# The order of GpSimd's queue around the last routed groups of a mixture-of-experts kernel

## The reference

```python
y = einsum('bct,bcd->bdt', x, cond_w[itok])        # 4096 tokens x 1024
logits = y @ W_gate + b_gate
_, top_idx = top_k(logits, 2)
y_all = relu(einsum('bsd,edh->bseh', y, W_e) + b_e)
out = x + take_along_axis(y_all, top_idx[..., None], axis=2).mean(axis=2)
```

## Time and profile before

| | us |
|---|---|
| median of 3 runs (893.49 to 895.28) | 893.74 |
| profiled execution | 893.59 |
| its span | 891.5 |
| TensorE busy | 851.7 |
| GpSimd busy | 511.1 |
| VectorE busy | 412.4 |
| ScalarE busy | 256.8 |

### The profile page before, as it was taken

One profiled execution on the slowest core, in us unless ns is written; L12 is line 12 of the kernel. 1 busy time (PEld: TensorE's weight loads), 2 busy tenths in 40 slices (PEclk: granted clock), 3 DMA queues, 4 the chain that ended last, 5 costly groups with the idle time before them and its releaser, 6 DMA issues.

```text
span 891.5 us, 16451 instructions
## 1 busy us (share of the span) xinstructions
PE 851.7 (96%) x4104; PEld 674.6 (76%) x4105; DVE 412.4 (46%) x548; ACT 256.8 (29%) x310; POOL 511.1 (57%) x559
## 2 busy tenths in 40 slices
PE   7899896999999999999999999999999999999992
PEld 3445475888878888888888888888888888888882
DVE  5688864356643373335533373336333733333320
ACT  5566310133511252113311331115111511222210
POOL 2266777767566756564665556555655566555411
PEclk9999997999999999999999999999999999999997
DMA  8999999878965586446854595547654564444333
GB/s 283 418 413 400 375 306 311 255 223 259 293 148 113 113 273 149 100 94 161 231 104 91 99 298 102 110 97 214 167 114 98 183 129 100 90 98 101 71 48 47
DMA packets 53065, 162.35 MB, mean 182 GB/s; under 512 B 13307, under 2 KB 13819, under 8 KB 53019
## 3 DMA queue, kind: packets, MB, share of 16 engines
q0 software_dynamic: 26464, 76.74, 40.0%
q1 hardware_dynamic: 20298, 67.91, 21.2%
q10 hardware_dynamic: 6272, 17.34, 4.9%
HBM read 106.73 MB, written 70.42 MB: 199 GB/s over the span
## 4 chain that ended last, share of the span: by engine, by line
PE 76%; DMA 14%; DVE 3%; issue 2%; POOL 2%; ACT 0%; POOLq 0%; ACTq 0%; SPq 0%; DVEq 0%
PE psO L573 73%; DMA rows<-in_x 5%; PE psO L513 2%; DMA out<-rows,first_to 1%; DMA out<-in_x 1%; DMA first<-slot_table 1%; DMA out<-ys,first_to 1%; DMA out<-ys,idx_s 1%; DMA slot_table<-toks,idx_all 1%; DMA rows<-y_rows,idx_g 1%; POOL slot_table L391 1%; POOL rows L419 1%; DVE turned L821 1%; DMA out<-rows,idx_s 1%; DMA wgc<-in_L_ffn_W_gate 1%
## 5 line engine op out<-in xcount | busy, mean ns | idle before, releaser
L573 PE MATMUL psO<-w_hi,a_hi 128*128 (+1 forms) x1104 | 342.0, 391 | 1.0 <-DVE a_lo L971 1.0
L573 PE MATMUL psO<-w_lo,a_hi 128*128 (+1 forms) x1104 | 340.8, 390 | 0.0
L573 PE MATMUL psO<-w_hi,a_lo 128*128 (+1 forms) x1104 | 340.4, 390 | 0.0
L419 POOL DMA_INDIRECT rows<-y_rows,idx_g x248 | 257.1, 1037 | 106.6 <-issue 52.4
L573 PEld LDWEIGHTS psO<-w_lo,a_hi 128*128 128x128 f32 x1104 | 207.8, 188 | 43.4
L573 PEld LDWEIGHTS psO<-w_hi,a_lo 128*128 128x128 f32 x1104 | 207.6, 188 | 43.3
L573 PEld LDWEIGHTS psO<-w_hi,a_hi 128*128 128x128 f32 x1104 | 207.0, 188 | 44.1 <-issue 1.8
L971 DVE TENSOR_TENSOR a_lo<-ys,a_hi 128x1024 fp32r<-128x1024 f32 x62 | 75.9, 1225 | 112.1 <-ACT a_hi L704 112.1
L692 ACT ACTIVATE ys<-ys 128x1024 f32<-128x1024 f32 x33 | 35.0, 1061 | 262.5 <-DVE ys L933 262.5
L692 ACT ACTIVATE rows<-rows 128x1024 f32<-128x1024 f32 x33 | 35.0, 1060 | 250.3 <-DVE rows L933 250.3
L933 DVE TENSOR_TENSOR ys<-psO,bias 128x1024 f32<-128x1024 f32 x33 | 40.3, 1222 | 130.9 <-PE psO L573 108.4
(11 more groups left out here) (129 smaller groups left out, 330.2 us busy)
## 6 DMA issues: line engine op xcount, KB each, us to landing
raw<-in_L_ffn_W_e SPq DMA_DIRECT2D x56, 512.0 KB, 6.3
rows<-in_x SPq DMA_DIRECT2D x32, 512.0 KB, 8.8
y_rows<-ys ACTq DMA_DIRECT2D x32, 512.0 KB, 8.7
out<-in_x SPq DMA_DIRECT2D x14, 1024.0 KB
bias<-in_L_ffn_b_e SPq DMA_DIRECT2D x8, 512.0 KB, 8.5
rows<-y_rows,idx_g POOLq DMA_INDIRECT x248
raw<-in_L_ffn_W_e POOLq DMA_DIRECT2D x4, 512.0 KB, 8.6
bias<-in_L_ffn_W_e POOLq DMA_DIRECT2D x4, 512.0 KB, 8.3
```

Source lines behind the costliest of these rows:

```text
L419: pool.indirect_dma_start(out=rows[:, slot, a * DQ:(a + 1) * DQ], out_offset=None, in_=y_parts[0:(1 + TOK) * Q, :], in_offset=bass.Indirec ...
L573: last = nc.tensor.matmul(ps[:, h * BANK:(h + 1) * BANK], a[:, p, k * P:(k + 1) * P], w[:, bass.ds(slot + (k * H + h * BANK), BANK)], star ...
```

## The change

No instruction is added or taken away; five programs are put in another order. GpSimd does the whole of route(3) ahead of early(0), then route(4) ahead of early(1) and so on, all seven early fetches and the gathers of tiles 7 and 8 ahead of any scatter, and then four scatters in a row. SP's reads for tiles 5 and 6 stand behind fewer copies. TensorE's share(5) and share(6) run at k = 5 of tiles 2 and 3. ScalarE loads the table ahead of relu(3) and early_hi(5). VectorE turns tile 4 ahead of finish_early(2), and its `schedule`, idx_all and finishes stand elsewhere among the early steps.

```diff
@@ sync
                 read_first(4)
-                for c in range(2, 7):
-                    copy(c)
+                copy(2)
+                copy(3)
                 read_first(5)
-                for c in range(7, 11):
+                for c in range(4, 8):
                     copy(c)
                 read_first(6)
-                for c in range(11, len(left)):
+                for c in range(8, len(left)):
                     copy(c)
@@ gpsimd
                 route(1)
                 route(2)
-                route(3, range(1))
+                route(3)
                 early(0)
-                route(3, range(1, 2))
+                route(4)
                 early(1)
-                route(4)
+                route(5)
                 early(2)
-                route(5)
+                route(6)
                 early(3)
-                pool.wait_ge(s_pad, 16)
-                scatter_early(0)
-                route(6)
                 early(4)
+                route(7)
                 early(5)
-                scatter_early(1)
-                route(7)
                 early(6)
-                scatter_early(2)
                 for s in range(G):
                     pool.wait_ge(s_xout[s], 16 * (len(STORES) // G))
                 pool.wait_ge(s_idx, 1)
                 gather(tile(0, EARLY))
                 gather(tile(0, EARLY + 1))
-                scatter_early(3)
+                pool.wait_ge(s_pad, 16)
+                for t in range(4):
+                    scatter_early(t)
                 regather(tile(0, 9))
@@ tensor
-                early_products(2, hooks={2: lambda: share(5)})
-                early_products(3)
-                early_products(4, hooks={0: lambda: share(6)})
+                early_products(2, hooks={5: lambda: share(5)})
+                early_products(3, hooks={5: lambda: share(6)})
+                early_products(4)
@@ scalar
                 early_hi(3)
+                early_hi(4)
                 relu(tile(0, 2))
-                early_hi(4)
-                relu(tile(0, 3))
-                early_hi(5)
                 for g in range(NG):
                     act.wait_ge(s_sc[g], LAND)
...
                                   slots_by).then_inc(s_tab, 16)
+                relu(tile(0, 3))
+                early_hi(5)
                 relu(tile(0, 4))
@@ vector
                 read_from(5)
-                schedule()
+                turn_early(4)
                 finish_early(2)
-                turn_early(4)
                 early_lo(4)
                 part(6)
+                schedule()
+                read_from(6)
                 finish_early(3)
-                read_from(6)
                 turn_early(5)
-                early_lo(5)
-                finish_early(4)
 
                 dve.wait_ge(s_tab, Q * 16)
...
                 dve.sem_inc(s_idx, 1)
+                early_lo(5)
                 dve.wait_ge(s_yout[1], 16 * NG)
...
                 dve.sem_inc(s_idx, 1)
+                finish_early(4)
                 turn_early(6)
```

## The result

The median is 907.8 us (903.84 to 908.71) beside 893.62 for the kernel before; the ratio is 1.0142, 95% interval 1.0114 to 1.0171. The profiled execution took 903.84 us with a span of 901.8; it is the shortest of the five on record (the fifth took 905.52). The direction was forecast, the size was not: +5.2 us was predicted, the profiled execution shows +10.3 and the median +14.2, above the range's 904.0. The 4 us between the profiled execution and the median have no profile, so what follows explains +10.3 and not +14.2.

What follows compares the result with a forecast made beforehand. TensorE, 96% busy and gapless from tile 12 on, was taken as the bound, so only tile 12's start counts: 255.19 to 260.4, +5.2 us, 893.6 + 5.2 = 898.8 us; range 894.6 to 904.0.

Steps and rivals of the forecast that it cites:

- TensorE's 8.2 us: TensorE's wait at share(5) in early tile 2, line 536; forecast to vanish, with 2.0 us of low clock.
- the wait at tile 3: A new TensorE wait ahead of tile 3, forecast at 1.2 us (0.9 to 3), TensorE starting at 146.4.
- that is all that can be won: TensorE's loss from tile 2 to tile 11, 11.9 us, taken as the most the change could win.
- the wait for three landings ahead of tile 8: VectorE's wait at line 1066, forecast to delay tile 8 to 210.2 and make TensorE wait 9.3 us.
- the drain: GpSimd's four scatters in a row, each waiting for earlier landings; forecast to start at 178.5, behind gather(8).
- A: The third scatter's landing, which VectorE waits for at line 1066; forecast at 199.4, bounds 197.3 to 203.3.
- dearer-drain rival: First two scatters land in 9.9 and 10.7 us as beside copies: A = 206.2, +12.0, 905.6 us; chance 0.11.
- The chain from A to tile 12: GpSimd's alternating scatters and gathers, forecast to put tile 12 at A + 61.0 = 260.4 instead of 255.19.
- the clock's price: 2.0 us of low clock after tile 8's wait, forecast to be covered by the 3.0 us wait at tile 9.
- its ledger: The check on +5.2 at tile 12: gone 8.2 + 2.0 + 1.0, come 1.2 + 9.3 + 2.0 + 3.0 + 1.6.
- short landings: Rival at line 433, scatters 1 and 2: landings of 4.4 us, A = 192.5, time 891.9 us; chance 0.07.
- the page's rule: A GpSimd DMA takes 2.0 us plus bytes at 436 GB/s: 3.2 us per scatter, 888.3 us; left out.

Runs made afterwards that it cites:

- e11: e2's kernel with route(6)'s second half behind early(3) and early_lo(5) ahead of VectorE's table wait; 891.98 us beside 896.36 for the kernel before.
- e12: Kernel before with only SP's order of copies and reads changed and share(5) at k = 5 of tile 2; 899.91 us beside 896.36.
- e2: Changed kernel with scatters 0, 1, 2 behind early(4), early(5), early(6), only scatter 3 behind gather 8; 892.71 us beside 893.84 for the kernel before.
- e4: Changed kernel with o_first moved in memory so VectorE waits for three landings only ahead of ahead(8); 909.23 us beside 905.5 for the changed kernel.
- e7: Changed kernel with SP's first weight loads for expert 1 held until scatter 0 landed, on another chip; 947.71 us, ratio 1.0158 to before.
- e1: The changed kernel run once more, unaltered, for a second profile; 905.5 us beside 893.84 for the kernel before.
- e3: Changed kernel with scatter 0 moved behind early(6), three scatters left in the row; 898.48 us beside 905.5 for the changed kernel.

## Why the prediction was wrong

- **TensorE's 8.2 us are removed: right,** and so is the wait at tile 3 (0.85 us, forecast 1.2; TensorE went on at 146.81, forecast 146.4). Not forecast: 1.6 us at share(6). The prediction's "that is all that can be won", 11.9 us, was not exceeded; the best form measured, e11, won 4.4, and e12 shows that taking the 8.2 us away by SP's order alone wins nothing.
- **The mechanism, the wait for three landings ahead of tile 8: right.** Tile 8 began 10.6 us after that wait's end (forecast 10.8). The wait on TensorE was 14.5 us and not 9.3: it ended 8.7 us later than forecast, and TensorE was ready 3.5 us later. e2 shows that the drain is the whole loss; e4 that gather 9 behind the drain holds the tiles at about the same place as VectorE's wait does.
- **The step that failed is A, the end of VectorE's wait: 208.3 and not 199.4.** The 8.9 us are four mis-sized terms. First, the drain began at 183.29 and not 178.5, 4.8 us: idx_all ended at 170.03 and not 165.0, as the last slot DMA started at 154.27 (forecast 152.4, single DMAs of GpSimd took 1.5 to 1.9 us instead of 0.97, and I counted one every 1.27), and the slots and the table took each about 1.5 us longer to land than I had allowed. SP's copies, which I had done near 155, were issued until 159.3, beside these landings; whether they are the reason was not tried. Second, the first landing took 9.6 us and not 7.5, 2.1 us: the loads beside it (e7, e4). The 7.5 came from a scatter that had such loads beside it too, but 6.5 us behind the first of them and not 4.4. I had named these loads as a point for the dearer-drain rival and not put them in the sum. Third, from a landing to the next issue 0.84 and 0.90 us passed, not 0.4, and to VectorE 1.5 us, not nothing: together 2.4. The second and third landings, 6.0 and 6.2 us, were 0.4 shorter than taken.
- **The chain from A to tile 12 was too long in the sum, 61.0 us against 56.7 measured** (265.05 - 208.32). Tile 9 did not wait: its rows were turned at A + 12.6 and not A + 15.0. Of these 2.4 us 0.8 are scatter 3, which started 0.5 us before VectorE went on and not 0.3 after, 0.3 are GpSimd's DMAs, where I had already taken off 1.1 for the long ones, and 1.3 are the landing, 5.5 us from the last DMA's start to the transpose and not 6.8. The clock's loss (10 matmuls' worth, 2.3 us and a little) stretched tile 8, so that from tile 8 on TensorE ran through: 10.6 + 43.5 for four tiles + 2.3 is 56.4 of the 56.7. So the clock's price, which I had let vanish in tile 9's wait, was paid. This error of -4.3 hid half of the one in A: 8.9 - 4.3 gives the 4.6 us by which tile 12 came later than forecast.
- **The range** took its bounds from the landings alone and gave the start of the drain, a sum of some sixty DMAs and two landings, only 2 us. That term alone was off by 4.8. (By the prediction's own 2 us the upper end would be 904.7 and not 904.0, and its ledger adds up to 5.9, which is 0.7 more than its +5.2.) That the profiled execution, 903.84, falls just inside the range is luck: the two errors above partly cancel. The case named "dearer drain", 905.6 us at 0.11, is where the kernel came out, though with one long landing and not two.
- **The rival "short landings" and the page's rule: no.** The Trainium skill's "DMA: Bandwidth & Descriptors", "Anatomy of one DMA", would have a 512 KB transfer land in 3.2 us, an estimate by that page. The two scatters without loads beside them took 6.0 and 6.2, so this trace disagrees with it for scatters that accumulate.

## What to carry to other kernels

When operations that must wait for one another's landings are taken out from between other work and put in a row, their landings, until then free, become the engine's time: here 24.5 us of queue from the first of four DMAs to the fourth. Before moving such a row, ask who else waits for its members (here another engine, through borrowed memory) and what stands behind it in the queue; both may hold the same place, and then mending one shows nothing. Taking the largest wait away from the bounding engine is worth its length only if nothing else comes late right behind it and the edit makes nothing else late.

## What was not expected of the hardware

- In the drains of the changed kernel, e1 and e3 a scatter of 512 KB that accumulates in DRAM landed in 5.8 to 6.3 us where no load was in flight when it was issued. With four 512 KB loads issued up to 5.4 us ahead it took 8.9 to 9.8 us (there, in e2 and in e4); the length moved with the loads from one scatter to another. It was not so each time: the changed kernel's scatter at 216.66, behind four loads issued 1.1 us apart from 209.59 on, landed in 6.5 us, and no run tells why.
- TensorE's clock did not follow the length of its idle time alone. After 2.19 us of idle time at tile 3 of e2 the granted clock was 0.50 (149.5 to 152.5 us) and the first matmul pair took 1.22 us; after 2.33 us at tile 12 of e4 it stayed 1.00 (269.9 to 272.5 us) and the pair took 0.72. After 3.46 us in e12 and 3.07 us in e11 only the first pair was quick, 0.73 us; the next ones took up to 1.05 us, where 0.62 is usual.
- Two chips ran the same kernel before in 925 to 945 us, two others in 892 to 899; what TensorE waited for on the first two the profile does not name.
